# Moving the expert splits, the scaled rows, the transposes and the halo copy inside one step of a pipelined RWKV and mixture-of-experts kernel

## The chip, the cores and the metric

The kernel runs on one core of one Trainium2 chip. The metric is the time of one launch in microseconds of device time. The kernel before took 1054.4 us (median of 3 runs, 1046.8 to 1061.9); one further execution was recorded by the profiler, and all rows come from that one.

## The reference, cut to what matters

```python
def _L0_attn_ref(x, ...):                   # one sequence of 4096 tokens, 256 channels
    xn = layer_norm(x, ln1_g, ln1_b)
    xx = token_shift(xn)                     # row t-1 beside row t
    xk, xv, xr = (xn * m + xx * (1.0 - m) for m in (mix_k, mix_v, mix_r))
    k, v = xk @ Wk.T, xv @ Wv.T
    sr = sigmoid(xr @ Wr.T)
    x = x + (sr * wkv(time_decay, time_first, k, v)) @ Wo.T     # a scan over the tokens
    xn2 = layer_norm(x, ln2_g, ln2_b)
    xk2, xr2 = ...                           # the same shift and mix again
    kv = square(relu(xk2 @ Wk_ffn.T)) @ Wv_ffn.T                # 256 -> 1024 -> 256
    return x + sigmoid(xr2 @ Wr_ffn.T) * kv

def _L0_ffn_ref(x, w1s, w2s, w3s, W1, W2, W3, Wg):
    shared = geglu(x, w1s, w2s, w3s)         # gelu(x @ w1) * (x @ w2) @ w3
    idx = argmax(x @ Wg)                     # one of 8 experts for each token
    return shared + geglu(x, W1[idx], W2[idx], W3[idx])

x = x + _layernorm(_L0_attn_ref(_layernorm(x)))
x = x + _layernorm(_L0_ffn_ref(_layernorm(x)))
```

## The kernel before

The 4096 tokens are worked in 16 chunks of 256. A software pipeline, `chunk_steps`, runs steps i = -1 to 17; step i works on chunk c0 = i (k, v, r projections and the scan), c1 = i - 1 (channel mix) and c2 = i - 2 (shared expert and expert choice), with the routed rows of c3 = i - 3 written out. Steps 6 to 13 are a hardware loop of two steps a turn, the others are written out. After step 17, `slot_steps` runs the 8 routed experts over 39 slots of 128 rows; the change does not touch it.

Each engine has its own program, and inside a step the order of its instructions is the order of the calls in the function `step` of that engine. Nothing is reordered: an instruction that waits for a semaphore holds everything behind it on its engine. The parts that matter here:

- TensorE. `projection(0)` (k) opens the step. It writes the PSUM bank `up[0]`, so it waits for `gu` of the previous step's third group of the shared expert. Then come `projection(1)`, `transpose_normed2`, `projection(2)`, `shared_down`, `shared_gate`/`shared_up` of groups 0 and 1 with `receptance` between, `transpose_next`, `channel_mix_up(0..3)`, `channel_mix_down`, `output`, and gate and up of groups 2 and 3. `channel_mix_up(q)` reuses the banks of the shared groups 0 and 1 and so waits for their Gelus (`gelu`) or products (`gu`).
- ScalarE. `ln0` (L667, `normed<-x_in`) writes the scaled rows of the next chunk; it waits for the inverse deviations `inv0` of GpSimd. `gelu` is L769, `sh_hi` L776, `mix_hi` L783, `relu_up` L748, `square` L756, `ln2` L667 (`normed<-x`), `xnT_norm` L661.
- VectorE. `mix2_lo` L1022, `kept`, `scan_b`, `scan_a` (L1045 to L1057), `shared(g)` (L1201, the product `gu` that TensorE waits for), `den_*` and `num*`, `halo` (L1000, one column), `gate`, `divide` (L1078), `mix0(m)` (L1006), `rw` (L1093), `x3_gate` (L1111), `x2_sum`, the moments, `shared(2)`, `x1_sum`, `shared(3)`.
- GpSimd. `inverse(n)` (L1459 to L1486), `difference` (L1500), two indirect writes (L1588), then in this order `sh_lo(0)`, `mix_lo(0)`, `mix_lo(1)`, `sh_lo(1)`, `inverse2`, `offset2`, `inverse1`, `mix_lo(2)` (L1547 is `sh_lo`, L1553 is `mix_lo`).

The expert splits. Every weight is used as two float16 parts. For the 8 experts' three matrices this is done beside the chunks: SyncE loads a matrix of float32 into `raw[m]` (L283), ScalarE writes the high part (`expert_hi`, L653), VectorE the low part (`expert_lo`, L981), both into a buffer `cut[m % 2]`, and SyncE stores the buffer to `w_split` in DRAM (L288). Matrices 0 and 2 of an expert share `cut[0]`; matrix 1 has `cut[1]`. In an even step matrix 0 of expert h - 1 gets its low part (`early_lo`), in an odd step matrix 2 (`early_lo`) and matrix 1 (`last_late`), so an odd step has two of them. ScalarE's high parts stand in the second half of a step: in an odd step one, between `mix_hi(0)` and `mix_hi(1)`, for matrix 0 of the next expert. It reuses `cut[0]`:

```python
if m == 0:                                   # expert_hi, ScalarE
    wait(act, S("expert_out2"), 16 * e)      # matrix 2 of expert e - 1 is stored
```

SyncE's own order in each step, which waits for VectorE where the comments say:

```python
for e, m in early_piece(i + 1, 1 - p, h + p) + late_piece(i + 1, 1 - p, h + p):
    load_expert(e, m)                        # waits for expert_lo{m} of expert e - 1
...
for e, m in early_piece(i, p, h) + last_late(i, p, h) + late_now(i, p, h):
    store_expert(e, m)                       # waits for expert_lo{m} of expert e
```

In an odd step that is: load matrix 0, load matrix 1 (which waits for the low part of matrix 1, the one of `last_late` in this same step), store matrix 2, store matrix 1.

## Time and profile before

| | us |
|---|---|
| median of 3 runs | 1054.4 |
| lowest and highest | 1046.8, 1061.9 |
| the profiled execution | 1044.2 |
| its span on the core | 1042.5 |
| mean granted TensorE clock of it | 0.97 of full |

The span is what the rows below count in, from its own zero; 1.7 us of the execution lie around it. A row of a timeline gives the start, the duration, the engine, the line of the kernel, the operation with the names that it writes and reads, and in brackets how long the engine had been idle and what ended that. Rows of one kind that follow each other are merged (x2, x4), and each overlaps the next by some 0.08 us. PE is TensorE, ACT ScalarE, DVE VectorE, POOL GpSimd, SPq the queue of SyncE.

### The profile page before, as it was taken

What the parts mean: (1) busy time and instruction counts of PE and PEld (TensorE: products, weight loads), DVE (VectorE), ACT (ScalarE), POOL (GpSimd) and SP (SyncE); (2) the same over time, 40 slices, a digit from 0 to 9 for tenths busy, and PEclk for the clock granted to TensorE, in tenths of its full rate; (3) what the DMA queues carried; (4) which work ended last, traced back from release to release, by engine and by line L of the source; (5) the groups of instructions that cost most, each with busy time, mean ns of one, the idle gap of its engine ahead of it and who ended that gap; (6) DMA issues with size and microseconds to landing.
All of it is one profiled execution on the core that took longest, in us unless ns stands there. A gap on an engine that the chain in (4) does not pass through costs nothing.

```text
span 1042.5 us, 28016 instructions
## 1 busy us (share of the span) xinstructions
PE 935.1 (90%) x9734; PEld 838.8 (80%) x9734; DVE 735.0 (71%) x1653; ACT 591.6 (57%) x1014; POOL 589.0 (56%) x800
## 2 busy tenths in 40 slices
PE   2366899999999999999999999869999999999994
PEld 1255788888878878878878887758999999999994
DVE  5887999999988988989889886432444444444442
ACT  5375787787777777776777774423333333333331
POOL 5346468567667667567567542443554554555453
PEclk9688999999999999999999999989999999999998
DMA  6111350351251350340343146566777788485510
GB/s 232 61 52 55 97 198 23 127 203 50 94 204 29 112 199 21 123 182 30 131 161 131 64 171 201 208 229 214 264 225 239 251 268 272 147 281 190 179 58 22
DMA packets 87339, 156.37 MB, mean 150 GB/s; under 512 B 5549, under 2 KB 68142, under 8 KB 82160
## 3 DMA queue, kind: packets, MB, share of 16 engines
q1 hardware_dynamic: 35760, 72.74, 20.3%
q10 hardware_dynamic: 46960, 65.89, 19.5%
q0 software_dynamic: 4560, 16.98, 4.2%
q8 instruction: 34, 0.56, 0.2%
q14 instruction: 25, 0.20, 0.1%
HBM read 178.35 MB, written 50.51 MB: 220 GB/s over the span
## 4 chain that ended last, share of the span: by engine, by line
PE 51%; DVE 16%; POOL 13%; issue 8%; ACT 6%; DMA 2%; ACTq 2%; SPq 1%; POOLq 0%; DVEq 0%
PE up L342 10%; PE up L344 10%; PE up L343 10%; PE yp L549 4%; PE yp L342 4%; PE yp L344 4%; PE yp L343 4%; PE yp L546 4%; POOL inv L1479 3%; DVE mixed L1006 2%; POOL inv L1466 2%; POOL sh_s L1547 2%; DVE stats L987 1%; ACT L769 1%; DVE arena L981 1%
## 5 line engine op out<-in xcount | busy, mean ns | idle before, releaser
L342 PE MATMUL up<-mix_s,arena 128*128 128x128 f16 x1248 | 211.1, 219 | 2.3 <-DMA arena<-w_split 1.8
L344 PE MATMUL up<-mix_s,arena 128*128 128x128 f16 x1248 | 211.1, 219 | 0.0
L343 PE MATMUL up<-mix_s,arena 128*128 128x128 f16 x1248 | 211.1, 219 | 0.0
L342 PE MATMUL up<-xf_s,arena 128*128 128x256 f16 x512 | 140.4, 274 | 5.5 <-issue 4.5
L344 PE MATMUL up<-xf_s,arena 128*128 128x256 f16 x512 | 140.5, 274 | 0.0
L343 PE MATMUL up<-xf_s,arena 128*128 128x256 f16 x512 | 140.4, 274 | 0.0
L1648 POOL TENSOR_TENSOR kf_s<-ex,kf_s 128x512 f16<-128x512 f32 x78 | 90.1, 1156 | 86.4 <-ACT kf_s L940 86.3
L1419 DVE SCALAR_TENSOR_TENSOR ex<-up,ex 128x512 f32<-128x512 f32 x78 | 53.9, 691 | 103.2 <-ACT ex L934 102.9
L342 PEld LDWEIGHTS up<-mix_s,arena 128*128 128x128 f16 x1248 | 122.0, 98 | 2.9 <-DMA arena<-w_split 1.9
L343 PEld LDWEIGHTS up<-mix_s,arena 128*128 128x128 f16 x1248 | 122.0, 98 | 0.4
L344 PEld LDWEIGHTS up<-mix_s,arena 128*128 128x128 f16 x1248 | 122.0, 98 | 0.0
L934 ACT ACTIVATE ex<-up 128x512 f32<-128x512 f32 x78 | 45.9, 589 | 104.1 <-issue 53.7
L1547 POOL TENSOR_TENSOR sh_s<-gu,sh_s 128x512 f16<-128x512 f32 x64 | 81.5, 1275 | 37.8 <-ACT sh_s L776 37.8
L940 ACT ACTIVATE kf_s<-ex 128x512 f16<-128x512 f32 x78 | 49.1, 630 | 80.3 <-DVE ex L1419 72.9
L1553 POOL TENSOR_TENSOR mix_s<-mixed,mix_s 128x512 f16<-128x512 f32 x48 | 62.1, 1295 | 46.3 <-ACT mix_s L783 46.3
L342 PE MATMUL up<-mix_s,w_fk 128*128 128x256 f16 x256 | 72.0, 281 | 15.3 <-ACT gu L769 12.8
L342 PE MATMUL yp<-arena,kf_s 128*128 128x256 f16 x312 | 85.1, 273 | 0.7 <-issue 0.7
L343 PE MATMUL yp<-arena,kf_s 128*128 128x256 f16 x312 | 85.1, 273 | 0.0
L344 PE MATMUL yp<-arena,kf_s 128*128 128x256 f16 x312 | 85.1, 273 | 0.0
L342 PE MATMUL yp<-arena,sh_s 128*128 128x256 f16 x256 | 71.6, 280 | 8.8 <-POOL sh_s L1547 8.8
L1006 DVE SCALAR_TENSOR_TENSOR mixed<-delta,vec,xnT 128x256 f32<-128x256 f32 x96 | 74.4, 814 | 1.2 <-POOL delta L1500 1.2
L769 ACT ACTIVATE gu<-up 128x512 f32<-128x512 f32 x64 | 36.6, 595 | 63.3 <-PE up L344 56.8
(228 smaller groups left out, 2904.2 us busy)
## 6 DMA issues: line engine op xcount, KB each, us to landing
arena<-w_split ACTq DMA_DIRECT2D x117, 1024.0 KB
arena<-in_W SPq DMA_DIRECT2D x24, 1024.0 KB, 6.0
w_split<-arena SPq DMA_DIRECT2D x24, 1024.0 KB, 10.2
rows<-routed_rows ACTq DMA_DIRECT2D x39, 261.0 KB, 2.9
routed_rows<-x_in SPq DMA_DIRECT2D x8, 650.0 KB, 6.4
normed<-routed_rows ACTq DMA_DIRECT2D x39, 128.0 KB, 2.5
x_in<-in_x SPq DMA_DIRECT2D x16, 256.0 KB, 2.8
x_res<-in_x SPq DMA_DIRECT2D x16, 256.0 KB, 2.7
```

The source lines that it names most:

```text
L342: pe.matmul(out, stat(0), mov(0), start=first, stop=False)
L343: pe.matmul(out, stat(0), mov(1), start=False, stop=False)
L344: return pe.matmul(out, stat(1), mov(0), start=False, stop=last)
L546: pe.matmul(yp[1][:, 0, :], kf[:, f, 0:P], w_fv[:, f, :], start=(f == 0), stop=(f == FT - 1))
L769: act.activation(gu[g % GUS][:], up[(3 + 2 * g) % 4][:], ACT.Gelu, scale=1 / WS).then_inc(S("gelu"), 1)
L934: act.activation(slot_g[q], up[2 * q][:].rearrange("p k n -> p (k n)"), ACT.Gelu, scale=1 / WS).then_inc(S("slot_gelu"), 1)
L940: act.activation(slot_h[b][:, 0, q * FT // 2:(q + 1) * FT // 2, :], slot_g[q].rearrange("p (f n) -> p f n", n=P), ACT.Copy).then_inc(S("sl ...
L1006: dve.scalar_tensor_tensor(out=mixed[m][:, k, :], in0=delta[:, k, :], scalar=vec[:, MK + m, k:k + 1], in1=x[:, k, 0:CH], op0=ALU.mult, op1 ...
L1419: dve.scalar_tensor_tensor(out=slot_g[q], in0=up[2 * q + 1][:].rearrange("p k n -> p (k n)"), scalar=HS / WS, in1=slot_g[q], op0=ALU.mult, ...
L1547: pool.tensor_tensor(sh_s[:, 1, 2 * g:2 * g + 2, :], gu[g % GUS][:], sh_s[:, 0, 2 * g:2 * g + 2, :], ALU.subtract).then_inc(S("sh_lo"), 1)
L1553: pool.tensor_tensor(mix_s[m][:, 1], mixed[m][:], mix_s[m][:, 0], ALU.subtract).then_inc(S("mix_lo"), 1)
L1648: pool.tensor_tensor(hs[:, 1], slot_g[q].rearrange("p (f n) -> p f n", n=P), hs[:, 0], ALU.subtract).then_inc(S("slot_h_lo"), 1)
```

## The change

On TensorE the transposes of the next chunk stand behind `channel_mix_up(1)` instead of ahead of `channel_mix_up(0)`. On ScalarE the scaled rows `ln0` stand behind the Gelus, and `xnT_norm` behind `relu_up(1)`. On VectorE `early_lo` moves from ahead of `mix2_lo` to behind `shared(1)`, `last_late` from behind `mix2_lo` to behind `mix0(1)`, `halo` from ahead of `gate` to just ahead of `divide`; in steps up to 2 `distances`, and in all steps the own-weight split `own(3)`, go ahead of `placing` and the first halo. SyncE and GpSimd keep their order.

```diff
                 shared_up(1)
+                channel_mix_up(0)
+                channel_mix_up(1)
                 transpose_next()
-                for q in range(4):
-                    channel_mix_up(q)
+                channel_mix_up(2)
+                channel_mix_up(3)
...
                 receptance()
-                if not at_step(i, -1):
-                    ln0(i + 1, 1 - p)
                 exps(1)
                 own(1)
                 gelu(0)
                 gelu(1)
-                xnT_norm()
+                if not at_step(i, -1):
+                    ln0(i + 1, 1 - p)
                 relu_up(0)
...
                 relu_up(1)
+                xnT_norm()
                 square(1)
...
                     tops(c0)
+                early = isinstance(i, int) and i <= 2
+                if on(c0) and early:
+                    distances(c0)
+                own(3)
...
-                if on(c0):
+                if on(c0) and not early:
                     distances(c0)
-                own(3)
...
-                else:
-                    early_lo(i, p, h)
                 if on(c1):
                     mix2_lo(c1, 1)
                     mix2_lo(c1, 0)
-                late_lo(last_late(i, p, h))
...
                 shared(0)
                 shared(1)
+                if not at_step(i, NC + 1):
+                    early_lo(i, p, h)
...
-                if on(i + 1):
-                    halo(xnT, i + 1, 1 - p, "halo", "xnT")
...
                     num(c0)
+                if on(i + 1):
+                    halo(xnT, i + 1, 1 - p, "halo", "xnT")
+                if on(c0):
                     divide(c0)
...
                     mix0(i + 1, 1 - p, 1)
+                late_lo(last_late(i, p, h))
                 if on(c1):
                     x3_gate(c1)
```

VectorE, odd step of the loop, from the split of the normed input to the first two products. `arena<-arena` is a low part of an expert, `gu<-up,gu` a product. Before:

```order
L1208 TENSOR_TENSOR xf_s<-tp,xf_s 128x512
L981 SCALAR_TENSOR_TENSOR arena<-arena 128x2048
L1022 TENSOR_TENSOR mix_s<-relu_k,mix_s 128x512
L1022 TENSOR_TENSOR mix_s<-relu_k,mix_s 128x512
L981 SCALAR_TENSOR_TENSOR arena<-arena 128x2048
L1045 TENSOR_TENSOR dist<-ex,val 128x512
L1050 SCALAR_TENSOR_TENSOR state<-ex,state 128x256 x2
L1057 SCALAR_TENSOR_TENSOR state<-ex,state,dist 128x256 x2
L1201 SCALAR_TENSOR_TENSOR gu<-up,gu 128x512
L1201 SCALAR_TENSOR_TENSOR gu<-up,gu 128x512
L1064 TENSOR_TENSOR mixed<-ex,state 128x512
```

The same place now, with line numbers two higher:

```order
L1210 TENSOR_TENSOR xf_s<-tp,xf_s 128x512
L1024 TENSOR_TENSOR mix_s<-relu_k,mix_s 128x512
L1024 TENSOR_TENSOR mix_s<-relu_k,mix_s 128x512
L1047 TENSOR_TENSOR dist<-ex,val 128x512
L1052 SCALAR_TENSOR_TENSOR state<-ex,state 128x256 x2
L1059 SCALAR_TENSOR_TENSOR state<-ex,state,dist 128x256 x2
L1203 SCALAR_TENSOR_TENSOR gu<-up,gu 128x512
L1203 SCALAR_TENSOR_TENSOR gu<-up,gu 128x512
L983 SCALAR_TENSOR_TENSOR arena<-arena 128x2048
L1066 TENSOR_TENSOR mixed<-ex,state 128x512
```

Two splits have left the stretch ahead of the products, and one stands right behind them. The other one, in the second half of the same step; `mixed<-delta,vec,xnT` is `mix0`, `er<-er` the divide. Before:

```order
L1078 RECIPROCAL er<-er 128x512
L1006 SCALAR_TENSOR_TENSOR mixed<-delta,vec,xnT 128x256 x2
L1093 TENSOR_TENSOR val<-val,er 128x512
L1006 SCALAR_TENSOR_TENSOR mixed<-delta,vec,xnT 128x256 x2
L1111 SCALAR_TENSOR_TENSOR gate_r<-gate_r,yp 128x512
```

Now:

```order
L1002 COPY xnT<-xnT 128x2
L1080 RECIPROCAL er<-er 128x512
L1008 SCALAR_TENSOR_TENSOR mixed<-delta,vec,xnT 128x256 x2
L1095 TENSOR_TENSOR val<-val,er 128x512
L1008 SCALAR_TENSOR_TENSOR mixed<-delta,vec,xnT 128x256 x2
L983 SCALAR_TENSOR_TENSOR arena<-arena 128x2048
L1113 SCALAR_TENSOR_TENSOR gate_r<-gate_r,yp 128x512
```

The second split now stands between `mix0(1)` and `x3_gate`, and the halo copy next to the divide. SyncE's queue in the odd step of the loop stands as it did; the names in brackets are the semaphores that it waits for, `expert_lo1` being the low part of matrix 1:

```order
L283 DMA arena<-in_W 128x2x1024
L283 DMA arena<-in_W 128x2x1024 [waits expert_lo1]
L288 ISA [waits expert_lo2]
L288 DMA w_split<-arena 128x4096
L288 ISA [waits expert_lo1]
L288 DMA w_split<-arena 128x4096
```

The store of matrix 2 is behind the load that waits for matrix 1, before and now.

## Rows read from the trace of the kernel before

**Rows 1.** The page, busy time, share of the span and instructions of TensorE.

```profile
PE 935.1 (90%) x9734; PEld 838.8 (80%) x9734; DVE 735.0 (71%) x1653; ACT 591.6 (57%) x1014; POOL 589.0 (56%) x800
```

**Rows 2.** Timeline of VectorE, the scan that opens steps 3, 7, 9 and 15.

```profile
129.11 1.35 DVE L1033 TENSOR_TENSOR_SCAN state<-neg_decay,state,up 128x256 f32<-128x256 f32 x2
...
281.29 1.37 DVE L1033 TENSOR_TENSOR_SCAN state<-neg_decay,state,up 128x256 f32<-128x256 f32 x2
...
360.65 1.37 DVE L1033 TENSOR_TENSOR_SCAN state<-neg_decay,state,up 128x256 f32<-128x256 f32 x2
...
597.26 1.38 DVE L1033 TENSOR_TENSOR_SCAN state<-neg_decay,state,up 128x256 f32<-128x256 f32 x2
```

**Rows 3.** Timeline of TensorE in steps 7 and 8.

```profile
299.30 0.27 PE L342 MATMUL up<-mix_s,w_fk 128*128 128x256 f16 x1 [2.29 <-ACT gu L769]
...
300.56 0.42 PE L343 MATMUL up<-mix_s,w_fk 128*128 128x256 f16 x1
...
320.08 0.27 PE L342 MATMUL up<-mix_s,w_k 128*128 128x256 f16 x1
...
322.71 0.43 PE L351 MATMUL tp<-ident,normed 128*128 128x128 f32 x2
...
337.22 0.49 PE L351 MATMUL tp<-ident,normed 128*128 128x128 f32 x3
...
338.26 0.28 PE L342 MATMUL up<-mix_s,w_fk 128*128 128x256 f16 x1 [0.45 <-ACT gu L769]
...
358.04 0.28 PE L342 MATMUL up<-mix_s,w_k 128*128 128x256 f16 x1 [0.49 <-DVE gu L1201]
```

**Rows 4.** Timeline of ScalarE in steps 2, 7 and 9.

```profile
101.38 1.09 ACT L667 ACTIVATE normed<-x_in,inv 128x256 f32<-128x256 f32 x2 [5.32 <-POOL inv L1481]
...
295.20 1.09 ACT L667 ACTIVATE normed<-x_in,inv 128x256 f32<-128x256 f32 x2 [3.90 <-POOL inv L1481]
...
298.56 1.08 ACT L769 ACTIVATE gu<-up 128x512 f32<-128x512 f32 x2
...
309.45 0.63 ACT L783 ACTIVATE mix_s<-mixed 128x512 f16<-128x512 f32 x1
309.97 1.91 ACT L653 ACTIVATE arena<-arena 128x2048 f16<-128x2048 f32 x1
...
359.63 1.09 ACT L667 ACTIVATE normed<-x,inv 128x256 f32<-128x256 f32 x2 [0.72 <-POOL inv L1469]
```

**Rows 5.** Timeline of VectorE in steps 7, 8 and 15.

```profile
299.18 0.69 DVE L1201 SCALAR_TENSOR_TENSOR gu<-up,gu 128x512 f32<-128x512 f32 x1 [2.21 <-ACT gu L769]
...
308.38 0.78 DVE L1006 SCALAR_TENSOR_TENSOR mixed<-delta,vec,xnT 128x256 f32<-128x256 f32 x2
...
309.69 2.67 DVE L1006 SCALAR_TENSOR_TENSOR mixed<-delta,vec,xnT 128x256 f32<-128x256 f32 x2
...
350.70 0.69 DVE L1111 SCALAR_TENSOR_TENSOR gate_r<-gate_r,yp 128x512 f32<-128x512 f32 x1 [1.04 <-PE yp L549]
...
357.29 0.69 DVE L1201 SCALAR_TENSOR_TENSOR gu<-up,gu 128x512 f32<-128x512 f32 x1
...
607.52 2.28 DVE L981 SCALAR_TENSOR_TENSOR arena<-arena 128x2048 f16<-128x2048 f32 x1
```

**Rows 6.** SyncE in step 15, the same step's first store alone, and all 24 stores.

```profile
596.20 14.00 SPq L283 DMA_DIRECT2D arena<-in_W  x2
610.24 0.47 SPq L288 DMA_DIRECT2D w_split<-arena  x1
...
w_split<-arena SPq DMA_DIRECT2D x1, 1024.0 KB, 8.6
...
DMA to landing us min/median/max: 3.9/10.2/14.6
```

**Rows 7.** Timeline of GpSimd at the end of step 8.

```profile
356.52 0.20 POOL L1459 TENSOR_TENSOR inv<-mv,eps_ws 128x2 f32<-128x2 f32 x1 [2.09 <-DVE mv L990]
...
359.55 1.16 POOL L1553 TENSOR_TENSOR mix_s<-mixed,mix_s 128x512 f16<-128x512 f32 x1
```

## The prediction

> **What bounds the kernel now.** I read the page first. TensorE is busy 90% of the span [rows 1], so up to the slots, which the change leaves alone, only idle time of TensorE can be won. Next I laid the steps side by side by the scan that opens each. Steps 3 to 14, twelve of them, take 597.26 - 129.11 = 468.2 us, and the two loop steps 7 and 8 together 360.65 - 281.29 = 79.36 [rows 2]. By TensorE's own rows the even step 8 takes 358.04 - 320.08 = 37.96; so the odd step 7 takes 41.4. In the even step TensorE is idle 0.45 ahead of the channel mix and 0.49 ahead of the next key projection [rows 3], which leaves about 37.0 of work; I use 36.9, since some 0.1 more is lost around the two gaps. That is the floor of a step. The odd step has a gap of 2.29 ahead of the channel mix, and behind it a matmul takes 0.42 where others take 0.27 [rows 3]: the engine runs at the lower of its two clock levels for a while. 41.4 - 36.9 - 2.3 leaves some 2 us, of which I count 1.6 to the clock and the rest to small gaps.
>
> Who causes the gap is in ScalarE's timeline: the scaled rows wait 3.90 us for GpSimd's inverse, and the Gelus stand behind them [rows 4]. VectorE's first product waits for the same Gelu 2.21 us [rows 5]. So the change attacks a true stall. But the row at 358.04 shows a second bound close by: TensorE waits there 0.49 us for VectorE's third product [rows 3]. VectorE's second half is already slightly late in an even step, and the change puts work into it.
>
> **The change part by part.** I count from the start of the key projection in a step, t = 0.
>
> Gelus ahead of the scaled rows. The 3.90 wait no longer holds the Gelus [rows 4]. The scaled rows now follow the Gelus, and TensorE asks for them only after two groups of the channel mix, so they cost nothing. What is late next is TensorE itself: it ends the up group 1 at 337.22 - 320.08 = 17.1, plus 0.2 for the last matmul [rows 3], and VectorE's second product, which needs that, starts at t = 17.4 in every step. It cannot be earlier.
>
> VectorE behind that product. In step 7 from the first product (299.18) to `mix0(1)` (309.69) pass 10.51 us without a wait on another engine; without the first product, 0.61, that is 9.90 [rows 5]. The order between is the same but for the halo copy, and an early split now stands in it. A split takes 2.28, 2.2 to the start of the next [rows 5]. So `mix0(1)` starts at 17.4 + 9.9 + 2.2 = 29.5. It took 2.67 there, while its twin at 308.38 took 0.78 [rows 5]: it takes turns with GpSimd's low parts. In the changed kernel the halo copy is later, so GpSimd's difference, its two indirect writes and its low parts all start later, and they meet `mix0(1)` again in both kinds of step. I take 2.6, bounded below by 0.8. It ends at t = 32.1.
>
> Even step. From `x3_gate` (350.70) to the end of the third product (357.29 + 0.69) are 7.28 [rows 5]. That gives 32.1 + 7.3 = 39.4 for the next key projection: 1.4 more than the 37.96 of now, though the Gelu stall is gone.
>
> Odd step. The late split follows `mix0(1)` and ends at 34.3. Here SyncE comes in. Its queue holds, in this order, the load of matrix 1, which needs this split, and the store of matrix 2. Step 15 shows that the order counts: SyncE stands 14.00 us in the two loads, and the store is issued at 610.24, only 0.44 behind the end of the second split (607.52 + 2.28 = 609.80) [rows 5, 6]. The first split of that step had long ended. The store lands 8.6 us after its issue [rows 6]. So in the changed kernel it lands at 34.3 + 0.4 + 8.6 = 43.4.
>
> Before, that did not matter: ScalarE's next high part started at 309.97 directly behind its neighbour [rows 4], with no idle, so the store had landed. Now it waits for 43.4. Queued behind it on ScalarE are the second scaled mix and the Gelu of group 2, then the rest of the step. High part 1.9, mix 0.5, Gelu 0.6 [rows 4], product 0.7 [rows 5]: 43.4 + 3.7 = 47.1 for the next key projection. I see no cover for this: TensorE has finished the step at 36.9 and VectorE is stopped at the product.
>
> It costs once more. GpSimd's low part of the mix waits for the same ScalarE, at t = 45.9, and the low part of a product and the inverses stand behind it. Two low parts of 1.16, overlapped, are 2.3 [rows 7]; from the start of the inverses (356.52) to the end of the normed rows (359.63 + 1.09) are 4.2 [rows 4, 7]. So the normed rows are ready at 52.4. TensorE would want them 322.71 - 320.08 = 2.6 after the key projection [rows 3], at 49.7. That is 2.7 more, and VectorE shifts along with it. The odd step then costs 47.1 + 2.6 = 49.7.
>
> A page speaks on the landing. The Trainium skill, "DMA: Bandwidth & Descriptors", section "Queues, rings and completion order", says that a later DMA of a queue need not complete after an earlier one. If the store of 1 MB did not suffer from the load in front of it, it could land as the fastest of the 24 did, in 3.9 us [rows 6], and the sum would be 7 x 4.7 = 33 us lower; the store of step 15, which has just this load in front, took 8.6, and that I follow. The same page, "Anatomy of one DMA", gives about 2.0 us plus the bytes at 436 GB/s, which would be an estimate of 6.8 us for both megabytes.
>
> The sum. Six pairs at 49.7 + 39.4 = 89.1 are 534.6 against 468.2: +66.4. Step 15 has the wait too, without mixes and without a key projection behind it; I take +6 for it (0 to +9). In the first steps ScalarE's wait of 5.32 in step 2 [rows 4] leaves the Gelus' way, and own-weight splits go ahead of a halo that waits anyway, while one expert split is added behind the products: I take -5 (-9 to 0). The tail and the slots: 0. Together +67. The profiled execution took 1044.2 us; with it that is 1111. The median of the runs shown is 10.2 higher, so I say 1122.
>
> Bounds. If `mix0(1)` met nothing of GpSimd, each of twelve steps would be 1.8 shorter, -22. A landing of 3.9 takes off 33; one of 14.6 would add 42, but that row is of a fuller queue, so I allow a third of it. TensorE's lower clock behind the new gaps may cost 1.6 again in each of up to twelve steps, though where it must wait for the normed rows anyway this is hidden; I allow 10.
>
> **The rivals.** First: SyncE and ScalarE are not held up (the store lands in time, or the high part has slack that I do not see), and only VectorE's chain is longer. Then an odd step ends at 34.3 + 7.3 = 41.6 and an even one at 39.4, 81.0 for the pair, six pairs 486: +18, less 5: 1067. For it: stores have landed in time in every loop step so far. Against it: the code order and the 14.00 us of step 15.
>
> Second, on the other side: the change makes the kernel faster. VectorE's second half is not on the path, because GpSimd's low parts fall into the divide and the stores land early; every step runs at TensorE's 36.9. Twelve steps take 443, -25, and with -5 of the first steps the time is 1024. It needs VectorE to do its work behind the second product in 36.9 - 17.4 = 19.5 us. The clean sum is 9.9 + 2.2 + 0.8 + 7.3 = 20.2 in the even step, where 7.3 still holds some 1.9 of meetings with GpSimd, and 2.2 more in the odd one. So the even step could do it and the odd one hardly.
>
> Third: the change does not do what it says, since the transposes or scaled rows are late and TensorE stops there instead. GpSimd's inverse came at 295.20, t = 16.5 in step 7 by the odd step's own start at 278.7, and TensorE wants the rows at 20; little speaks for it. It would leave about 1054.
>
> **How the numbers follow.** My forecast has a chance of 0.79, the VectorE rival 0.12, the faster one 0.06, the third 0.03. A measurement tells 2% of this kernel, 21 us, from no change. The forecast lies over that but for a sliver of 0.01, the first rival and the third within it, with 0.03 of the first above: faster 0.06, within 2% 0.13, slower 0.81. The forecast's own range is 1088 to 1150; to take in part of the first rival I go down to 1068.
>
> **What would show it.** In the changed profile: odd steps near 50 us and even ones near 39; the high part L655 of odd steps with ScalarE idle some 10 us before it, released by the DMA `w_split<-arena`; no wait of the scaled rows that holds a Gelu; SyncE's loads standing until the late split ends; TensorE waiting for `gu` at the key projection in both kinds of step, and for the normed rows behind odd ones. If ScalarE has no such idle time, my main term is wrong. If even steps come to 37, my view of the meetings with GpSimd is.

## The result and the profile after

The changed kernel takes 1113.26 us, median of four runs (1111.7 to 1114.76); the kernel before took 1055.49 beside it (1046.81 to 1061.86; the three runs of the table above and one more). The ratio is 1.0553, with a 95% interval from 1.0474 to 1.0632. The forecast was 1122.

The page of the changed kernel, its span, busy times, granted TensorE clock in 40 slices, and the costliest idle time of ScalarE:

```profile
span 1112.9 us, 28016 instructions
...
PE 949.7 (85%) x9734; PEld 845.7 (76%) x9734; DVE 750.2 (67%) x1653; ACT 586.7 (53%) x1014; POOL 523.2 (47%) x800
...
PEclk9688999998998998998999899898999999999998
...
L655 ACT ACTIVATE arena<-arena 128x2048 f16<-128x2048 f32 x24 | 45.6, 1902 | 90.4 <-DMA w_split<-arena 90.4
```

TensorE's busy time grew by 14.6 [rows 1] and the span by 70, so most of the loss is waiting. The last line names the wait that grew: ScalarE stood 90.4 us in all ahead of high parts, and what ended that was a store. GpSimd's busy time fell from 589.0 to 523.2 [rows 1] although it does the same work; what the trace shows of that stands in the last section.

The timeline of VectorE, the scans that open steps 3, 7, 8, 9 and 15, against [rows 2]:

```profile
123.23 1.35 DVE L1035 TENSOR_TENSOR_SCAN state<-neg_decay,state,up 128x256 f32<-128x256 f32 x2
...
301.66 1.37 DVE L1035 TENSOR_TENSOR_SCAN state<-neg_decay,state,up 128x256 f32<-128x256 f32 x2
...
351.32 1.37 DVE L1035 TENSOR_TENSOR_SCAN state<-neg_decay,state,up 128x256 f32<-128x256 f32 x2
390.95 1.37 DVE L1035 TENSOR_TENSOR_SCAN state<-neg_decay,state,up 128x256 f32<-128x256 f32 x2
...
659.02 1.37 DVE L1035 TENSOR_TENSOR_SCAN state<-neg_decay,state,up 128x256 f32<-128x256 f32 x2
```

The odd step 7 takes 49.66, the even step 8 takes 39.63, and the twelve steps 535.8 against 468.2. Step 3 begins 5.9 sooner. From here on t is the time since the key projection of step 7 began, at 299.05. TensorE's timeline, its gaps in steps 7 and 8, against [rows 3]:

```profile
299.05 0.28 PE L342 MATMUL up<-mix_s,w_k 128*128 128x256 f16 x1 [1.65 <-DVE gu L1203]
...
329.73 1.13 PE L562 MATMUL yp<-w_o,val 128*128 128x256 f32 x4 [0.68 <-DVE val L1095]
...
346.17 0.40 PE L342 MATMUL up<-mix_s,w_k 128*128 128x256 f16 x1 [9.21 <-DVE gu L1203]
...
351.53 0.65 PE L351 MATMUL tp<-ident,normed 128*128 128x128 f32 x4 [0.76 <-ACT normed L669]
...
388.35 0.28 PE L342 MATMUL up<-mix_s,w_k 128*128 128x256 f16 x1 [1.66 <-DVE gu L1203]
```

The gap of 2.29 ahead of the channel mix is gone. In its place stand gaps of 9.21 at the key projection behind the odd step, 1.65 and 1.66 behind the even ones, and 0.68 ahead of the output (`yp<-w_o,val`). To see what held the product, follow one step through four engines. First VectorE, in step 7, against [rows 5]:

```profile
316.57 0.69 DVE L1203 SCALAR_TENSOR_TENSOR gu<-up,gu 128x512 f32<-128x512 f32 x1 [0.42 <-PE up L344]
317.18 2.28 DVE L983 SCALAR_TENSOR_TENSOR arena<-arena 128x2048 f16<-128x2048 f32 x1
...
326.91 2.16 DVE L1008 SCALAR_TENSOR_TENSOR mixed<-delta,vec,xnT 128x256 f32<-128x256 f32 x2
...
329.60 1.77 DVE L1008 SCALAR_TENSOR_TENSOR mixed<-delta,vec,xnT 128x256 f32<-128x256 f32 x2
331.29 2.28 DVE L983 SCALAR_TENSOR_TENSOR arena<-arena 128x2048 f16<-128x2048 f32 x1
...
345.42 0.69 DVE L1203 SCALAR_TENSOR_TENSOR gu<-up,gu 128x512 f32<-128x512 f32 x1 [7.09 <-ACT gu L771]
```

The late split ends at 333.57, and SyncE's queue waits for it. SyncE in steps 6 and 7, against [rows 6]:

```profile
277.28 0.37 SPq L283 DMA_DIRECT2D arena<-in_W  x1
280.08 0.38 SPq L288 DMA_DIRECT2D w_split<-arena  x1
...
316.71 17.25 SPq L283 DMA_DIRECT2D arena<-in_W  x2
334.19 0.37 SPq L288 DMA_DIRECT2D w_split<-arena  x1
```

In the even step load and store follow each other by 2.8 us. In the odd one the queue stands in its two loads for 17.25, and the store of matrix 2 is issued at 334.19, though its split was done at 319.46. ScalarE in step 7, against [rows 4]:

```profile
342.48 1.91 ACT L655 ACTIVATE arena<-arena 128x2048 f16<-128x2048 f32 x1 [12.74 <-DMA w_split<-arena]
344.29 0.61 ACT L785 ACTIVATE mix_s<-mixed 128x512 f16<-128x512 f32 x1
344.81 0.58 ACT L771 ACTIVATE gu<-up 128x512 f32<-128x512 f32 x1
```

The store landed 8.3 us after its issue; the Gelu that VectorE's product and then TensorE want is the third instruction behind that wait. GpSimd, in step 7, against [rows 7]:

```profile
309.11 0.20 POOL L1485 TENSOR_TENSOR inv<-inv 128x2 f32<-128x2 f32 x1
...
327.61 1.17 POOL L1553 TENSOR_TENSOR sh_s<-gu,sh_s 128x512 f16<-128x512 f32 x1
329.81 1.27 POOL L1559 TENSOR_TENSOR mix_s<-mixed,mix_s 128x512 f16<-128x512 f32 x1 [1.03 <-ACT mix_s L785]
344.98 1.15 POOL L1559 TENSOR_TENSOR mix_s<-mixed,mix_s 128x512 f16<-128x512 f32 x1 [13.90 <-ACT mix_s L785]
```

GpSimd stands behind ScalarE too, so the inverses for the normed rows are late; that is the 0.76 ahead of the transposes at 351.53. Its low parts at 327.61 and 329.81 lie beside VectorE's `mix0(0)` and `mix0(1)`.

### The profile page after: what moved, and what is told of

Same layout as the page of the kernel before. It is cut to its first block, busy times and chain, and to the rows that moved or that the text cites. A ratio compares the mean times of both kernels' runs of the same rounds, so it can differ in the third digit from the quotient of the medians.

```text
span 1112.9 us, 28016 instructions
## 1 busy us (share of the span) xinstructions
PE 949.7 (85%) x9734; PEld 845.7 (76%) x9734; DVE 750.2 (67%) x1653; ACT 586.7 (53%) x1014; POOL 523.2 (47%) x800
## 4 chain that ended last, share of the span: by engine, by line
PE 42%; DVE 21%; issue 15%; ACTq 8%; POOL 6%; DMA 4%; ACT 4%; DVEq 0%; POOLq 0%; SPq 0%
PE up L342 8%; PE up L344 8%; PE up L343 8%; PE yp L342 5%; PE yp L344 5%; PE yp L343 5%; DVE mixed L1008 4%; DVE arena L983 4%; ACTq L881 3%; DMA w_split<-arena 2%; PE tp L351 2%; DMA arena<-w_split 2%; ACTq L901 1%; DVE er L1080 1%; ACTq L884 1%
## 5 line engine op out<-in xcount | busy, mean ns | idle before, releaser
L655 ACT ACTIVATE arena<-arena 128x2048 f16<-128x2048 f32 x24 | 45.6, 1902 | 90.4 <-DMA w_split<-arena 90.4
L1203 DVE SCALAR_TENSOR_TENSOR gu<-up,gu 128x512 f32<-128x512 f32 x64 | 43.4, 679 | 72.2 <-ACT gu L771 58.0
L1553 POOL TENSOR_TENSOR sh_s<-gu,sh_s 128x512 f16<-128x512 f32 x64 | 77.4, 1211 | 22.4 <-ACT sh_s L778 22.1
L1008 DVE SCALAR_TENSOR_TENSOR mixed<-delta,vec,xnT 128x256 f32<-128x256 f32 x96 | 85.2, 928 | 1.2 <-POOL delta L1506 1.2
L342 PE MATMUL up<-mix_s,w_k 128*128 128x256 f16 x64 | 21.4, 334 | 73.8 <-DVE gu L1203 48.5
```

Of the source, the lines that this page charges most:

```text
L342: pe.matmul(out, stat(0), mov(0), start=first, stop=False)
L655: act.activation(cut[m % 2][:, 0, :], raw[m], ACT.Copy, scale=WS).then_inc(S("expert_hi"), 1)
L1008: dve.scalar_tensor_tensor(out=mixed[m][:, k, :], in0=delta[:, k, :], scalar=vec[:, MK + m, k:k + 1], in1=x[:, k, 0:CH], op0=ALU.mult, op1 ...
L1553: pool.tensor_tensor(sh_s[:, 1, 2 * g:2 * g + 2, :], gu[g % GUS][:], sh_s[:, 0, 2 * g:2 * g + 2, :], ALU.subtract).then_inc(S("sh_lo"), 1)
```

## The experiments

"Sum" is the start of step 15 less that of step 3, by VectorE's scan in the profiled execution of each kernel; ratios are to the kernel before, with their 95% interval. The ratios compare across groups of runs better than the times do, as the kernel before had medians of 1055.5 (beside the changed kernel), 1047.5 (beside late_back, store_first, both_back and late_only), 1051.2 (sooner, halo_early, ln0_only, early_only) and 1046.25 us (the other four), while the expectations in us start from 1055. Where an interval lies wholly on one side of 1, the direction holds; by the whole of their interval only the changed kernel, late_only, ln0_and_own and two_orders are over 2% from the kernel before.

| kernel | ratio | step 3 at | step 15 at | sum |
|---|---|---|---|---|
| before | 1 | 129.11 | 597.26 | 468.2 |
| changed | 1.0553 (1.0474 to 1.0632) | 123.23 | 659.02 | 535.8 |
| late_back | 1.0048 (1.0023 to 1.0073) | 121.77 | 605.06 | 483.3 |
| store_first | 1.0140 (1.0084 to 1.0196) | 120.81 | 615.61 | 494.8 |
| both_back | 0.9770 (0.9714 to 0.9826) | 121.11 | 575.21 | 454.1 |
| late_only | 1.0498 (1.0438 to 1.0559) | 130.12 | 651.67 | 521.6 |
| late_store_first | 0.9927 (0.9895 to 0.9958) | 127.71 | 593.21 | 465.5 |
| early_only | 1.0003 (0.9967 to 1.0040) | 131.58 | 603.22 | 471.6 |
| ln0_only | 0.9820 (0.9748 to 0.9893) | 127.39 | 579.07 | 451.7 |
| ln0_and_early | 1.0019 (0.9985 to 1.0052) | 131.38 | 603.01 | 471.6 |
| halo_early | 0.9872 (0.9804 to 0.9940) | 121.83 | 580.62 | 458.8 |
| sooner | 0.9799 (0.9743 to 0.9855) | 123.06 | 577.58 | 454.5 |
| ln0_and_own | 0.9743 (0.9695 to 0.9792) | 126.08 | 579.70 | 453.6 |
| two_orders | 0.9713 (0.9662 to 0.9763) | 120.40 | 573.27 | 452.9 |

**late_back.** The changed kernel with the late split where it was before.

```diff
                     mix2_lo(c1, 0)
+                late_lo(last_late(i, p, h))
...
                     mix0(i + 1, 1 - p, 1)
-                late_lo(last_late(i, p, h))
```

> The changed kernel with the late split (matrix 1) back behind the second low part of the second mix, as before; the early split stays behind the second product. My theory: SyncE's queue is free early again, ScalarE's high part has its store in time, so the 12.7 us idle of ScalarE in odd steps goes, and what is left is VectorE's longer second half, the same in both kinds of step: odd 39.4 instead of 49.7, even 39.4. Six pairs 473 instead of 536, step 15 five less: about 1045 us (1030 to 1060). Rival (the late split costs only its own 2.2 us on VectorE, the store is not its doing): 1113 - 6 x 2.2 = 1100, with ScalarE's idle time still there.

Measured: 1052.26 us. In the steps 3 to 15 no wait of ScalarE for a store is left. One of 3.8 us stays further on, at 670; the kernel before has the same one. Even steps take 39.6 (39.4 said); odd ones take 41.0, 1.6 more than said and 1.4 more than the even ones. The rows of TensorE in step 7 of this kernel show where these 1.4 are:

```profile
312.50 1.78 PE L562 MATMUL yp<-w_o,val 128*128 128x256 f32 x7 [1.47 <-DVE val L1095]
...
321.38 0.28 PE L342 MATMUL up<-mix_s,w_k 128*128 128x256 f16 x1 [1.65 <-DVE gu L1203]
```

The gap ahead of the output is 1.47, where the even step has 0.67, and there is one of 0.48 ahead of the channel mix; together they are 1.3 of the 1.4. An odd step has a second split in its first half, and VectorE begins the second half later by it. The place of this one instruction is worth 535.8 - 483.3 = 52.5 us in the twelve steps. The rival, 1100 with the wait still there, is out.

**store_first.** VectorE's order of the changed kernel, and only SyncE's queue in another order.

```diff
-                for e, m in early_piece(i + 1, 1 - p, h + p) + late_piece(i + 1, 1 - p, h + p):
+                for e, m in early_piece(i + 1, 1 - p, h + p):
+                    load_expert(e, m)
+                for e, m in early_piece(i, p, h):
+                    store_expert(e, m)
+                for e, m in late_piece(i + 1, 1 - p, h + p):
                     load_expert(e, m)
...
-                for e, m in early_piece(i, p, h) + last_late(i, p, h) + late_now(i, p, h):
+                for e, m in last_late(i, p, h) + late_now(i, p, h):
                     store_expert(e, m)
```

> The changed kernel with VectorE's order untouched; only SyncE's queue is reordered: the store of the early matrix (0 or 2) is issued ahead of the load of matrix 1 and no longer stands behind a load that waits for the late split. My theory: the store is issued about 14 us sooner and has landed when ScalarE wants its buffer, so ScalarE's idle time goes; odd steps fall from 49.7 to VectorE's bound 34.3 + 7.3 = 41.6, even ones stay at 39.4. Six pairs 486, step 15 five less: about 1059 us (1045 to 1070). Rival A (it is VectorE's two splits in the second half that make the time, the queue's order does not matter): no change, 1113. Rival B (a store that is alone in the queue still lands late because its split itself is late): ScalarE idle between 2 and 8 us, 1075 to 1100.

Measured: 1061.97 us. SyncE of this kernel in the odd step 9:

```profile
384.10 0.37 SPq L283 DMA_DIRECT2D arena<-in_W  x1
387.02 0.37 SPq L288 DMA_DIRECT2D w_split<-arena  x1
400.97 0.37 SPq L283 DMA_DIRECT2D arena<-in_W  x1
401.64 0.37 SPq L288 DMA_DIRECT2D w_split<-arena  x1
```

The store goes out at 387.02, right behind its split, and the load that waits for the late split comes after it. No wait of ScalarE for a store is left, so rival B is out. In the twelve steps 41 us are gained with no engine's work changed: the block was the queue's order. Rival A is out too. Odd steps take 41.3 on average (41.6 said). Even steps, though, take 41.15, not 39.4. TensorE of this kernel at the end of step 7 shows why:

```profile
325.39 0.28 PE L346 MATMUL up<-mix_s,w_k 128*128 128x256 f16 x1 [3.26 <-DVE gu L1207]
...
325.94 0.42 PE L348 MATMUL up<-mix_s,w_k 128*128 128x256 f16 x1
```

Behind a gap of 3.26 the matmuls go from 0.28 to 0.42 us, up to 329.5, and the granted clock of that stretch is 0.53, near the lower of the two levels. Here nothing covers that loss, and it lands in the even step: in step 8 VectorE's second product starts 19.0 us behind the key projection, in step 7 17.5. Six even steps are 1.75 over, less 0.3 for each of six odd ones: that is the 8.8 us by which the sum is over the expected 486.

**both_back.** Late_back, and the early split ahead of the second mix's low parts as well.

```diff
                     last_slots()
+                else:
+                    early_lo(i, p, h)
...
                 shared(1)
-                if not at_step(i, NC + 1):
-                    early_lo(i, p, h)
```

> The changed kernel with both splits back in the first half of the step, where they were before; the scaled rows behind the Gelus, the later transposes, the later halo and the early own splits stay. My theory: the splits alone made the loss; without them mix0(1) ends at 29.9, the next key projection can come at 37.2, and the Gelu stall of odd steps is gone too: twelve steps of about 37.2 = 446 instead of 536, step 15 and first steps as said: about 1020 us (1010 to 1035), faster than before. Rival (the rest of the change is no gain, because GpSimd's later low parts and the later normed rows take it back): about 1050 to 1060.

Measured: 1023.9 us, 2.3% less than before. Even steps take 36.5 to 37.5, odd ones 37.3 to 39.7. The rival, no gain at all, is out. What remains of the change is a gain, and the two moved splits are the loss, all of it.

**late_only.** One line of the change alone, on the kernel before.

```diff
                     mix2_lo(c1, 0)
-                late_lo(last_late(i, p, h))
...
+                late_lo(last_late(i, p, h))
                 if on(c1):
                     x3_gate(c1)
```

> The kernel before with nothing but the late split moved behind mix0(1). My theory: this one line is enough for SyncE's block: the store of matrix 2 is issued at t = 36, lands at 45, high part, mix, Gelu and product 3.7 behind it, normed rows 2 more: odd steps about 50 instead of 41.4, even ones 38 as before. Six times 9 and 5 for step 15: about 1115 us (1100 to 1125). Rival (VectorE's chain only): odd steps 2.2 longer, 1055 + 13 = 1068.

Measured: 1100.22 us; odd steps 47.5 to 49.4, even ones 37.6 to 38.1 but for one of 42.1. The wait of ScalarE, from the list of waits of this kernel (us in total, times, longest):

```profile
ACT arena L653 <- DMA w_split<-arena: 90.6, 7, 13.8
```

Seven waits with the total that the changed kernel has. The expectation was 15 us too high; 8 of these are the median of the kernel before in this group, the rest odd steps that came out up to 2.5 shorter than 50.

**late_store_first.** Late_only with the queue of store_first.

```diff
-                for e, m in early_piece(i + 1, 1 - p, h + p) + late_piece(i + 1, 1 - p, h + p):
+                for e, m in early_piece(i + 1, 1 - p, h + p):
+                    load_expert(e, m)
+                for e, m in early_piece(i, p, h):
+                    store_expert(e, m)
+                for e, m in late_piece(i + 1, 1 - p, h + p):
                     load_expert(e, m)
...
-                for e, m in early_piece(i, p, h) + last_late(i, p, h) + late_now(i, p, h):
+                for e, m in last_late(i, p, h) + late_now(i, p, h):
                     store_expert(e, m)
...
                     mix2_lo(c1, 0)
-                late_lo(last_late(i, p, h))
...
                     mix0(i + 1, 1 - p, 1)
+                late_lo(last_late(i, p, h))
```

> late_only (ratio 1.050: the kernel before with the late split behind mix0(1)) with SyncE's queue reordered, the store of the early matrix ahead of the load of matrix 1. My theory: SyncE's block is all but the whole of late_only's 5%. Store landed in time, ScalarE's idle ahead of the high part gone; VectorE has taken 2.2 us out of the first half of the odd step, which ends the Gelu stall as in early_only, and put it into the second: odd steps 39 to 41, even ones 38: ratio 0.995 (0.985 to 1.005). Rival: the late split costs by VectorE's chain: above 1.015.

Measured: 1040.26 us. Without the block the same move of the split is a small gain on the kernel before, 0.7%. So of late_only's 5.0% the queue is more than all. Of the Gelu stall a part stays, as one split still stands ahead of the second mix's low parts: in step 7 the scaled rows wait 1.68 (3.90 before) and TensorE 0.56 (2.29 before).

**early_only.** The early split alone behind the products, on the kernel before.

```diff
                     last_slots()
-                else:
-                    early_lo(i, p, h)
...
                 shared(1)
+                if not at_step(i, NC + 1):
+                    early_lo(i, p, h)
```

> The kernel before with one part alone: the early split (matrix 0 or 2) behind the second product; the late one stays in the first half. My theory: no queue is blocked, since the load of matrix 1 waits only for the late split; VectorE's second half, which sets the key projection in even steps (0.49 us late already), gets 2.2 longer: even steps 40.2; odd ones, where VectorE had a little to spare, 42.5. 6 x (2.2 + 1.2) = +20: ratio about 1.019 (1.01 to 1.03). Rival: the first half, freed of 2.2 us, ends sooner and pays for it: ratio 1.00. Rival: ScalarE waits for the store of this matrix too, since its split is now 10 us later: ratio 1.05.

Measured: 1050.0 us, no change. My theory fell for the odd step. The scans of steps 7, 8 and 9 of this kernel:

```profile
288.53 1.37 DVE L1033 TENSOR_TENSOR_SCAN state<-neg_decay,state,up 128x256 f32<-128x256 f32 x2
328.55 1.38 DVE L1033 TENSOR_TENSOR_SCAN state<-neg_decay,state,up 128x256 f32<-128x256 f32 x2
367.25 1.37 DVE L1033 TENSOR_TENSOR_SCAN state<-neg_decay,state,up 128x256 f32<-128x256 f32 x2
```

The odd step 7 takes 40.0 (41.2 before, 42.5 expected) and the even one 38.7 (38.1 before, 40.2 expected); the sum is 3.4 longer, the total the same. In step 7, where the kernel before loses 2.3 us to the Gelus, taking the split out of the first half ended the stall. GpSimd and ScalarE there:

```profile
295.98 0.20 POOL L1479 TENSOR_TENSOR inv<-inv 128x2 f32<-128x2 f32 x1
```

```profile
298.44 1.08 ACT L667 ACTIVATE normed<-x_in,inv 128x256 f32<-128x256 f32 x2
```

The scaled rows wait for nothing, where they waited 3.90 [rows 4]. The first rival, that the freed first half pays for the longer second one, is what came out.

**ln0_only.** ScalarE's scaled rows behind the Gelus, alone, on the kernel before.

```diff
                 receptance()
-                if not at_step(i, -1):
-                    ln0(i + 1, 1 - p)
                 exps(1)
                 own(1)
                 gelu(0)
                 gelu(1)
+                if not at_step(i, -1):
+                    ln0(i + 1, 1 - p)
```

> The kernel before with one part of the change alone: ScalarE's scaled rows behind the two Gelus. TensorE's transposes stay ahead of the channel mix and VectorE's halo where it was. My theory: the Gelu stall of odd steps (2.3 us of TensorE, and the lower clock behind it) goes, and TensorE now asks for the scaled rows when the last is just ready, with 0 to 1 us lost; odd steps from 41.3 to 39 or so, even ones the same: 6 x 2 and the first steps 5: ratio about 0.983 (0.975 to 0.99). Rival: the wait only moves from the channel mix to the transposes in front of it, as GpSimd's inverse is still what comes last: ratio 1.00.

Measured: 1027.71 us. This one edit has the shortest sum of all, 451.7. In its step 7 TensorE waits 0.68 us ahead of the channel mix, for VectorE's product, where it waited 2.29 for the Gelu. ScalarE waits for stores in this kernel too, 14.2 us in seven waits, the longest 4.0; what they cost no run separates.

**ln0_and_early.** Both of the last two edits.

> ln0_only with the early split behind the second product too: the cell that is missing between ln0_only (0.982) and early_only (1.000). In early_only the odd steps went from 41.3 to 38.7 and the even ones from 38.1 to 40.0: taking the split out of the first half freed GpSimd's inverse and ended the Gelu stall as the moved scaled rows do, and the 2.2 us in the second half took it back. My theory: both cure the same stall, so together they don't add; the price stays in every step: 39.5 to 40 in even steps, 39 to 41 in odd ones, about 1045 to 1055, ratio 1.00. Rival: the price was a matter of even steps alone: 0.99.

(The text on record has the two kinds of step of early_only crossed: the odd ones are those of 40.0, the even ones those of 38.7.) Measured: 1050.25 us, and a sum of 471.6, that of early_only to the tenth; steps of 40.1 and 38.7. The two edits end the same stall, and against ln0_only the early split costs 19.9 us in twelve steps, 1.7 in each. The rival, a price in even steps alone, is out.

**halo_early.** Both_back with the halo copy at its place of before.

```diff
                 own(0)
+                if on(i + 1):
+                    halo(xnT, i + 1, 1 - p, "halo", "xnT")
...
                     num(c0)
-                if on(i + 1):
-                    halo(xnT, i + 1, 1 - p, "halo", "xnT")
```

> The kernel both_back with the halo copy back at its place of before, ahead of the gate; the transposes and ScalarE's rows stay late. My theory: in both_back ScalarE gives the rows at 331.4 and VectorE would come to this place at 329.5, so it stands 1.9 us in most steps and, being what sets the key projection, hands that on: 12 steps x 1.5 to 1.9 = 18 to 23 us more than both_back's 1024: 1044 (1035 to 1050). Rival: the wait is covered, and GpSimd's sooner difference pays for it: 1024 or less.

Measured: 1033.47 us. VectorE's list of waits in this kernel:

```profile
DVE xnT L1002 <- ACT xnT L663: 18.6, 13, 2.5
```

13 waits of 1.4 on average; a quarter of the 18.6 shows in the sum (458.8 against 454.1). The direction was right, the size was not. The rival named what pays back most of it: in the twelve steps VectorE's busy time is 423.8 where both_back has 433.4, and the `mix0` rows (L1008) take 57.4 in place of 70.8. In step 7 the first of them takes 0.78, not 2.17: GpSimd's low part is done before it starts.

**sooner.** Both_back with the transposes one group earlier, ScalarE's rows behind the first relu, and the halo behind the gate.

```diff
                 channel_mix_up(0)
-                channel_mix_up(1)
                 transpose_next()
+                channel_mix_up(1)
...
                 relu_up(0)
+                xnT_norm()
...
                     gate(c2)
+                if on(i + 1):
+                    halo(xnT, i + 1, 1 - p, "halo", "xnT")
...
```

> Both splits in the first half, and the rows of the next chunk one group sooner: TensorE transposes behind the first group of the channel mix, ScalarE normalises them right behind the first relu, VectorE copies the halo behind the gate, 1.2 us sooner than in both_back. GpSimd's difference, indirect writes and low part of the product then come sooner and leave mix0(0), which took 2.16 for two in both_back, to VectorE. My theory: VectorE's second half gets 1 us shorter and still sets the key projection, so steps go from 37.5 and 38.6 to 37.0 and 37.7: about 1014 us (1006 to 1022). Rival: the meetings with GpSimd only move to other instructions (the later low parts), no change from both_back: 1024. Second rival: TensorE waits for the scaled rows at the earlier transposes (they were ready at 326.4, TensorE asks at 328.1, so 1.7 to spare in an odd step): slower than both_back.

Measured: 1027.3 us (1019.96 to 1029.36), sum 454.5: no gain over both_back (454.1). Neither rival fits. The meetings did not only move: in the twelve steps L1008 takes 64.9 where both_back has 70.8. TensorE waits for the scaled rows 0.2 us in them. The gain went into other waits: VectorE stands 7.3 us for TensorE's channel mix (`gate_r`, L1113) where it stood 2.3, and 5.2 for the shared expert's up groups where it stood 3.5. Which of the three moves does that, no run separates.

**ln0_and_own.** Ln0_only, and in the first steps the distances and own splits ahead of the halo.

```diff
                 if on(c0):
                     tops(c0)
+                early = isinstance(i, int) and i <= 2
+                if on(c0) and early:
+                    distances(c0)
+                own(3)
...
-                if on(c0):
+                if on(c0) and not early:
                     distances(c0)
-                own(3)
```

> ln0_only (the kernel before with the scaled rows behind the Gelus), and of the rest of the change only that in the first steps the distances and the own-weight splits go ahead of the halo of the second mix. Both expert splits, the transposes and the next halo stay as before. My theory: the two gains add. both_back reached its step 3 at 121.1 where ln0_only reached it at 127.4; its steps 3 to 14 were no shorter than those of ln0_only (454 and 452 us). So 1026 - 5 = about 1021, ratio 0.977 (0.970 to 0.984), not slower than any version so far. Rival: the six us of the first steps came from the later transposes: no gain over ln0_only, ratio 0.982.

Measured: 1023.23 us (1019.66 to 1028.52).

**two_orders.** Ln0_and_own, with the late transposes, ScalarE's rows and the halo of the change in the steps up to 2 alone.

```diff
-                transpose_next()
+                early = isinstance(i, int) and i <= 2
+                if not early:
+                    transpose_next()
                 for q in range(4):
                     channel_mix_up(q)
+                    if q == 1 and early:
+                        transpose_next()
...
```

> ln0_and_own, and in the first steps (up to step 2) also the transposes behind two groups of the channel mix, ScalarE's rows and the halo late, as the change has them; from step 3 on the order of before for these three. My theory: ln0_only had 4.25 us of TensorE idle at the transposes at 60.4, where both_back had 0.63 at 62.3; with the late order that goes too. Step 3 starts at about 121 and the later steps take 452: 1019 us, ratio 0.975 (0.968 to 0.982). Rival: own splits alone give all of it, so no difference from ln0_and_own.

Measured: 1019.95 us (1015.81 to 1024.68), on the same chip as ln0_and_own. The two can't be told apart by their times, but by their traces: step 3 starts at 126.08 in ln0_and_own and at 120.40 in two_orders. Of the seven us between ln0_only (127.39) and two_orders, the own splits give 1.3 and the three late moves together (transposes, ScalarE's rows, halo) 5.7. The transposes in step 1 of ln0_only, and then of two_orders:

```profile
64.68 1.11 PE L351 MATMUL tp<-ident,normed 128*128 128x128 f32 x4 [4.25 <-ACT normed L667]
```

```profile
62.88 0.66 PE L351 MATMUL tp<-ident,normed 128*128 128x128 f32 x4 [1.34 <-ACT normed L671]
```

In ln0_and_own, with the own splits alone, this wait is still 3.99.

Two_orders beats both kernels: 2.9% less than before (2.4 to 3.4), and with it the changed one.

## Why the prediction was right, and where its sizes were off

The loss. The changed kernel is both_back times 1.080. The early split in the second half is 1.0048 / 0.9770, 2.8%; the late one 1.0553 / 1.0048, 5.0%, of which the queue's order is 1.0553 / 1.0140, 4.1%. The 0.9% left is VectorE's longer second half with what TensorE's clock loses behind its gap. (Each ratio has up to 0.8% of uncertainty. Taken on the kernel before, the queue's order is 1.0498 / 0.9927, 5.8%: the shares depend on what stands beside them.) This is the prediction's sum in its parts: a longer chain of VectorE in every step, and SyncE's block in odd ones.

Step by step, at t from 299.05. The second product starts at 17.5 (17.4 said). The late split ends at 34.5 (34.3), the store is issued at 35.1 (34.7) and has landed at 43.4 (43.4), the key projection comes at 47.1 (47.1), the transposes of the normed rows at 52.5 (52.4). Odd steps 49.7, even ones 39.6 (39.4), the sum 535.8 (534.6), the first steps -5.9 (-5), step 15 +5.2 (+6): its gap of TensorE closes 43.1 us into the step, where it was 37.9 before.

The page of the Trainium skill that was weighed, "DMA: Bandwidth & Descriptors", section "Queues, rings and completion order", allows a later DMA to complete ahead of an earlier one. Here the store took 8.3 us to land with a load issued 0.6 ahead of it, near the 8.6 of [rows 6] and not the 3.9; the measured row decided rightly. The formula behind the prediction's 6.8 us stands in the Trainium skill for DMAs that GpSimd issues, while these are SyncE's, and the measured 8.3 lies above it.

What was off:

- The median. I added 10.2 us to the sum by the profile, since the profiled execution of before lay that far under the median shown. The changed kernel has no such distance: its profiled execution took 1114.8, its median is 1113.3. The distance was scatter of the kernel before (15 us between its runs). By the profile the sum was 1111, 3.6 under that execution. So the miss of 9 us is this term and the 1.5 by which the changed kernel's execution lies over its median, less the 3.6.
- The tail, put at 0. First steps, twelve steps and step 15 are -5.9 + 67.6 + 5.2 = 66.9 of the 70.4 us by which the span grew; 3.5 come behind step 15's gap. There TensorE has waited 9.18 us and gets a granted clock of 0.55 from 702.2 to 709, and from the transposes at 702.11 to the up groups at 711.37 it takes 9.3 us, where the kernel before takes 6.4 at full clock.
- The meeting with GpSimd. I gave `mix0(1)` 2.6 and `mix0(0)` nothing. They took 1.77 and 2.16. The sum is near (3.9 for 3.4) by luck, the place was wrong, and the forecast had no gap there: the 2.16 sit ahead of the receptance-weighted value, and TensorE waits some 0.7 for it at the output in each step.
- ScalarE's idle time: "some 10", measured 12.74. Its end was right; ScalarE was done with its work 2.7 sooner than I had it.
- The 2.6 behind the odd step. It is there (346.17 to 351.53 are 5.36, against 2.63 in [rows 3]), but only 0.76 of it as a gap. The rest is the lower clock behind the 9.21 gap: the row at 346.17 takes 0.40, and the granted clock up to 349.9 is 0.50. As foreseen, it costs nothing more where the normed rows are late anyway. In store_first they are not late, and there the second product of the even step comes 1.5 later.
- The first steps. The size, 5.9 for 5, was right in part by luck: I named the Gelus and the own splits, but ln0_only gives 1.7 at step 3, the own splits 1.3, and the late transposes with the rows and the halo, which I had put at nothing, 5.7. In the changed kernel the moved splits take back a part of that (123.23, against 121.11 in both_back).

What stayed open: why late_only's odd steps scatter from 47.5 to 49.4, and what ScalarE's waits for stores cost in ln0_only.

## What to carry to other kernels

A queue of DMA issues is an engine too: when an instruction is moved to a later place, look at every issue that waits for it and at everything behind that in the queue; putting the store ahead of the load that waits was worth 41 us here. Before moving work out of a stretch that stalls into one that does not, find what stalls it: an edit that only reorders the waiting instruction (ln0_only, -1.8%) took the stall away for nothing, while the move of 2.2 us of work paid it back in full (early_only, 0.0%). And two cures of one stall do not add.

## What the runs showed of the hardware

A GpSimd instruction of two elements per partition, 0.20 us alone, is held by VectorE's splits and by what follows them. In the kernel before, step 7, VectorE and GpSimd:

```profile
288.10 2.27 DVE L981 SCALAR_TENSOR_TENSOR arena<-arena 128x2048 f16<-128x2048 f32 x1
290.30 1.28 DVE L1022 TENSOR_TENSOR mix_s<-relu_k,mix_s 128x512 f16<-128x512 f32 x2
291.50 2.28 DVE L981 SCALAR_TENSOR_TENSOR arena<-arena 128x2048 f16<-128x2048 f32 x1
293.70 0.68 DVE L1045 TENSOR_TENSOR dist<-ex,val 128x512 f32<-128x512 f32 x1
```

```profile
288.75 5.69 POOL L1479 TENSOR_TENSOR inv<-inv 128x2 f32<-128x2 f32 x1
```

It starts beside the first split and ends at 294.44, 0.06 behind the last of five VectorE instructions in a row; the scaled rows, which waited 3.90 us [rows 4], start at 295.20. In two_orders, step 7, its neighbour L1487 takes 6.36 and ends 0.06 behind the same five. The Trainium skill, "SBUF — State Buffer", section "SBUF: two separate sides", says that an operation of VectorE with two SBUF inputs and one of GpSimd exclude each other for a whole instruction. All five have two such inputs, and the direction agrees; but by that rule alone the wait could end with the first split, at 290.37. It ended only with the fifth. What keeps GpSimd out between them, no run shows. Over the whole run, from the groups of GpSimd's instructions before, and then of the changed kernel:

```profile
L1479 POOL TENSOR_TENSOR inv<-inv 128x2 f32<-128x2 f32 x16 | 47.2, 2949 | 1.3
```

```profile
L1485 POOL TENSOR_TENSOR inv<-inv 128x2 f32<-128x2 f32 x16 | 3.4, 213 | 1.3
```

It is the same instruction under its new line number, and 44 of the 66 us by which GpSimd's busy time fell. This is what made the scaled rows late in the kernel before. Taking a split away shortened it: with one split ahead of the two low parts (late_store_first, step 7) the instruction takes 3.49; with the only split behind them (early_only, step 7) the chain of small instructions is done at 296.45, before that split begins at 297.84, and the same instruction takes 0.20.

TensorE's clock. After TensorE had been idle for 9.21 (changed), 7.99 (late_only) and 3.26 us (store_first), the granted clock was 0.50 to 0.53 for a while, the lower of its two levels, and 1.00 again after that. In the changed kernel these stretches lasted 2.7 to 5.3 us. Behind the gap of 2.29 that the kernel before has in steps 7, 9, 11 and 13 it fell in three, to 0.50 to 0.53 [rows 3 for step 7], and stayed at 1.00 in step 13. Behind the gaps of 1.65 in late_back and early_only it stayed at 1.00.
